# A chunked delta rule: the triangular solve folded into the tables, and four scan links a chunk in place of six

## The chip, the cores and the metric

One core of one Trainium2 chip runs the whole program. The metric is device microseconds (us) of one execution; lower is better.

## The reference, cut to what matters

The program is a block of a small network: gated experts, a delta-rule attention, gated experts, a prototype mixture, a helical attention, a prototype mixture. The change touches the delta-rule attention alone. With 2 batches of 16 heads (32 pairs), 2048 tokens and head size 16, it computes for each pair:

```python
def step(S, inp):
    qt, kt, vt, at, bt = inp
    v_hat = jnp.einsum('bij,bi->bj', S, kt)
    err = vt - v_hat
    S = at[:, None, None] * S + bt[:, None, None] * (kt[:, :, None] * err[:, None, :])
    o = jnp.einsum('bij,bi->bj', S, qt)
    return (S, o)
```

`S` is 16x16 for a pair; k and q are normalised, `at` is the decay (alpha) and `bt` the step size (beta).

## The kernel before

The tokens are cut into chunks of 8 (`CHUNK`, `C`). What depends on k, q, alpha and beta alone is computed ahead, for all chunks, in the stage `delta_chunks`; the stage `delta_recurrence` (its tiles are named `delta_scan_...`) then runs through the 256 chunks in order. Between them lies `delta_record` in DRAM, one record per chunk and pair. A record before holds five tables and a decay, 513 numbers: SOLVE (8x8, the inverse of a triangular matrix), MIX (8x8), K_IN (8x16), K_OUT (16x8), Q_IN (8x16) and the chunk's decay.

**The chunk stage.** The 128 partitions hold 2 batches x 4 parts of time x 16 heads. Each partition has 512 tokens, taken in 4 units of 128 tokens (`UNIT`); a unit has N = 16 chunks and is stored in 2 runs of 8 chunks. Per unit:

- SP loads k and q of the next unit (16 DMAs) once ACT has turned those of this one, and then stores the records, 8 DMAs a run.
- ACT turns k and q to token order (L1665), copies k to PSUM (`k_bank`, L1673), later copies SOLVE and the decay into the record.
- The scalar products of each token's k or q with the earlier k of its chunk are made by rows (w, t): w is 0 for k and 1 for q, t the token; the row has t + w products of 16 numbers for each of 16 chunks, so 256 (t + w) elements. GpSimd (POOL) multiplies 11 of the 15 rows (L1606) into three slots of `terms`; DVE sums each into `gram` (L1708), and multiplies and sums the other 4 rows itself, with k from `k_bank`.
- POOL also makes K_IN and Q_IN (L1651). DVE makes the decay products `g` (L1704, 8 small instructions), K_OUT (L1736), the triangular inverse (`invert`, L1746 to L1755) and MIX (L1760).

**The scan.** The partitions hold 2 batches x 64, four partitions of a head with 4 columns of S each (`JQ`). 32 rounds of 8 chunks; a hardware loop (`Fori`) runs over pairs of rounds. DVE runs the chain: 6 links a chunk, each in two lanes (halves of the columns) that alternate, so 12 instructions:

- links 0 and 1: product of K_IN with the state (L1949), sum with the value to `error` (L1961);
- links 2 and 3: product of SOLVE with `error`, sum to `u` (L1965);
- links 4 and 5: product of K_OUT with `u`, sum with the decayed state to the new `state` (L1969).

A link of one lane waits for the link before it of the same lane (the semaphore `chain`). Beside it ACT makes the decayed state that the last link adds (L1893), copies the state (L1896) and `u` (L1898) to SBUF for POOL, and in the sixth chunk of a round (`LOOK = 5`) copies out the outputs of the round before (L1885). POOL makes 512 products for the output from the state and Q_IN (L1931), 256 from `u` and MIX (L1935), and adds the 24 terms of an output in pairs to 12 (L1942, `o_halves`). When a round is done, PE adds those 12 with 12 matmuls against the identity (L1867; the profile records each f32 matmul as two instructions). SP loads the round after next once the round is done, and stores the outputs.

A stage ends with a barrier of all engines; the next one starts only then.

## Time and profile before

| | us |
|---|---|
| median of 3 runs | 5048.27 (5047.78 to 5050.8) |
| the profiled execution, its own time | 5050.58 |
| its span in the profile | 5048.8 |
| DVE busy over the span | 4012.5 |
| PE busy over the span | 3644.2 |
| ACT busy over the span | 3071.2 |
| POOL busy over the span | 2040.4 |
| mean granted TensorE clock, share of full | 0.86 |

The own time is what the runs are timed by; the span is what the profile's rows add up to. Shares of busy time are averages over stages that have different limits, so a change in one stage is read from the rows of that stage.

### The profile page before, as it was taken

What the parts mean: (1) busy time and instruction counts of PE and PEld (TensorE: products, weight loads), DVE (VectorE), ACT (ScalarE), POOL (GpSimd) and SP (SyncE); (2) the same over time, 40 slices, a digit from 0 to 9 for tenths busy, and PEclk for the clock granted to TensorE, in tenths of its full rate; (3) what the DMA queues carried; (4) which work ended last, traced back from release to release, by engine and by line L of the source; (5) the groups of instructions that cost most, each with busy time, mean ns of one, the idle gap of its engine ahead of it and who ended that gap; (6) DMA issues with size and microseconds to landing.
All of it is one profiled execution on the core that took longest, in us unless ns stands there. A gap on an engine that the chain in (4) does not pass through costs nothing. (4 is left out here: it accounts for less than half of the span.)

```text
span 5048.8 us, 65143 instructions
## 1 busy us (share of the span) xinstructions
PE 3644.2 (72%) x15374; PEld 1330.5 (26%) x15374; DVE 4012.5 (79%) x6760; ACT 3071.2 (61%) x4256; POOL 2040.4 (40%) x2075
## 2 busy tenths in 40 slices
PE   7985002322222589788859999999999999999568
PEld 3431001211221234234212222222222222222123
DVE  5536869999999566337879999999999999998352
ACT  5567212222222256334738999999999999999342
POOL 1000657777777211111733444444444444444112
PEclk9998556666666799899979999999999999999789
DMA  1014653433333200002450111111111111110300
GB/s 44 8 46 108 108 124 76 91 78 77 85 84 76 72 11 7 10 8 85 169 146 20 37 37 37 36 36 37 37 37 37 37 36 34 36 25 5 108 10 33
DMA packets 126522, 276.18 MB, mean 55 GB/s; under 512 B 41297, under 2 KB 70865, under 8 KB 117905
## 3 DMA queue, kind: packets, MB, share of 16 engines
q1 hardware_dynamic: 124208, 263.05, 21.8%
q10 hardware_dynamic: 1952, 9.18, 0.6%
q8 instruction: 122, 2.00, 0.2%
q14 instruction: 240, 1.96, 0.1%
HBM read 178.65 MB, written 93.36 MB: 54 GB/s over the span
## 5 line engine op out<-in xcount | busy, mean ns | idle before, releaser
L1032 POOL TENSOR_TENSOR att_heads_rest<-att_heads_probs,att_heads_high 128x352 f16<-128x352 f32 x1024 | 872.6, 852 | 1226.4 <-DVE att_heads_rest L1184 1165.9
L1164 DVE TENSOR_REDUCE att_heads_maxima<-att_heads_peek 128x1 f32<-128x1024 f32 x992 | 1210.0, 1220 | 26.4 <-PE att_heads_peek L1059 26.4
L1132 ACT ACTIVATE att_heads_probs<-att_heads_scores 128x1024 f32<-128x1024 f32 x1024 | 1057.7, 1033 | 155.1 <-PE att_heads_scores L1078 137.8
L1078 PE MATMUL att_heads_scores<-att_heads_q,att_heads_k 128*128 128x512 f16 (+1 forms) x4096 | 1072.1, 384 | 21.0 <-issue 17.5
L1134 ACT ACTIVATE att_heads_high<-att_heads_scores 128x1024 f16<-128x1024 f32 x1024 | 1056.3, 1032 | 0.0
L1184 DVE TENSOR_TENSOR att_heads_rest<-att_heads_probs,att_heads_high 128x672 f16<-128x672 f32 x1024 | 885.3, 865 | 65.7 <-POOL att_heads_rest L1032 54.5
L1867 PE MATMUL delta_scan_sums<-delta_scan_o_halves,main_identity 128*128 128x256 f32 x768 | 247.0, 496 | 952.5 <-POOL delta_scan_o_halves L1942 952.5
L1059 PE MATMUL att_heads_peek<-att_heads_k,att_heads_q 112*128 112x512 f16 x1984 | 597.8, 382 | 17.7 <-DVE att_heads_maxima L1164 14.9
L1078 PEld LDWEIGHTS att_heads_scores<-att_heads_q,att_heads_k 128*128 128x128 f16 (+1 forms) x4096 | 319.0, 98 | 691.6 <-issue 443.1
L1867 PEld LDWEIGHTS delta_scan_sums<-delta_scan_o_halves,main_identity 128*128 128x128 f32 x768 | 194.7, 259 | 1005.2 <-POOL delta_scan_o_halves L1942 965.8
L1094 PE MATMUL att_heads_out<-att_heads_high,att_heads_v_head 128*64 128x512 f16 x2048 | 418.1, 405 | 14.8 <-DVE att_heads_rest L1184 14.2
L1094 PE MATMUL att_heads_out<-att_heads_rest,att_heads_v_head 128*64 128x512 f16 x2048 | 393.6, 381 | 0.0
L259 PE MATMUL ffn_pre<-ffn_xn_parts,ffn_weights 128*128 128x512 f16 x1536 | 335.7, 382 | 11.9 <-POOL ffn_weights L298 11.9
L1931 POOL TENSOR_TENSOR delta_scan_o_terms<-delta_scan_state_copy,delta_scan_record 128x512 f32<-128x512 f32 x256 | 301.5, 1178 | 87.3 <-ACT delta_scan_state_copy L1896 87.3
L1898 ACT ACTIVATE delta_scan_u_copy<-delta_scan_banks 128x32 f32<-128x32 f32 x256 | 50.5, 197 | 436.1 <-DVE delta_scan_s_terms L1949 434.1
L341 DVE SCALAR_TENSOR_TENSOR main_x<-ffn_hidden,ffn_gate,main_x 128x512 f32<-128x512 f32 x256 | 194.9, 764 | 151.3 <-ACT ffn_hidden L284 151.3
L1893 ACT ACTIVATE delta_scan_s_terms<-delta_scan_banks,delta_scan_record 128x64 f32<-128x64 f32 x256 | 96.6, 377 | 306.0 <-DVE delta_scan_terms L1949 305.9
L1942 POOL TENSOR_TENSOR delta_scan_o_halves<-delta_scan_o_terms 128x384 f32<-128x384 f32 x256 | 256.2, 1001 | 22.7 <-POOL delta_scan_o_terms L1935 5.1
L284 ACT ACTIVATE ffn_hidden<-ffn_pre,ffn_expert 128x512 f32<-128x512 f32 x256 | 175.4, 687 | 138.7 <-PE ffn_pre L259 136.9
L1606 POOL TENSOR_TENSOR delta_chunks_terms<-delta_chunks_kq 128x256 f32<-128x256 f32 (+6 forms) x44 | 101.8, 2355 | 361.7 <-ACT delta_chunks_kq L1665 342.3
L1949 DVE TENSOR_TENSOR delta_scan_terms<-delta_scan_record,delta_scan_banks 128x256 f32<-128x256 f32 x512 | 199.6, 450 | 53.2 <-issue 39.1
L1935 POOL TENSOR_TENSOR delta_scan_o_terms<-delta_scan_u_copy,delta_scan_record 128x256 f32<-128x256 f32 x256 | 174.3, 681 | 156.0 <-ACT delta_scan_u_copy L1898 156.0
(251 smaller groups left out, 5104.3 us busy)
## 6 DMA issues: line engine op xcount, KB each, us to landing
delta_scan_record<-delta_record SPq DMA_DIRECT2D x64, 1026.0 KB, 10.7
att_heads_q<-att_hel SPq DMA_DIRECT2D x192, 128.0 KB, 3.1
att_heads_k<-att_hel SPq DMA_DIRECT2D x192, 128.0 KB, 3.2
delta_record<-delta_chunks_record SPq DMA_DIRECT2D x64, 256.5 KB, 4.7
att_hel<-att_hel_high SPq DMA_DIRECT2D x32, 512.0 KB, 4.4
att_hel<-att_hel_rest SPq DMA_DIRECT2D x32, 512.0 KB, 5.0
att_o<-att_heads_out_copy SPq DMA_DIRECT2D x256, 32.0 KB
att_out_parts<-att_o ACTq DMA_DIRECT2D x8, 1024.0 KB, 15.8
```

Of the source, the lines that this page charges most:

```text
L259: mm = nc.tensor.matmul(pre[:, k % SLOTS], weights[:, u, w_part, tile, o * P:(o + 1) * P], xn_parts[:, x_part, tile, tokens(n)], start=til ...
L1032: nc.gpsimd.tensor_tensor(rest[:, step % 4, SPLIT:], probs[:, step % 4, SPLIT:], high[:, step % 4, SPLIT:], ALU.subtract).then_inc(rest_b_ ...
L1059: mm = nc.tensor.matmul(peek[:, j], q[0:MAX_ROW, slot, 0, tile * P:(tile + 1) * P], k[0:MAX_ROW, slot, 0, tokens(part * 2 + j)], start=Tru ...
L1078: mm = nc.tensor.matmul(scores[:, step % 2, tokens(j)], k[0:rows, slot, number, tile * P:(tile + 1) * P], q[0:rows, slot, number, tokens(h ...
L1094: mm = nc.tensor.matmul(out[j * WIDE:(j + 1) * WIDE, half], v_head[:, slot, tile], part[:, step % 4, tokens(j)], start=tile == 0 and part ...
L1132: nc.scalar.activation(probs[:, step % 4], scores[:, step % 2], ACT.Exp, scale=LOGIT_SCALE).then_inc(probs_ready, 1)
L1134: nc.scalar.activation(high[:, step % 4], scores[:, step % 2], ACT.Exp, scale=LOGIT_SCALE).then_inc(high_ready, 1)
L1164: nc.vector.tensor_reduce(maxima[:, m:m + 1], peek[:].rearrange("p j n -> p (j n)"), AX.X, ALU.max).then_inc(peek_read, 1)
L1184: nc.vector.tensor_tensor(rest[:, step % 4, 0:SPLIT], probs[:, step % 4, 0:SPLIT], high[:, step % 4, 0:SPLIT], ALU.subtract).then_inc(rest ...
L1867: mm = nc.tensor.matmul(sums[:, 0:COLUMNS], c["identity"][:], o_halves[:, slot, e].rearrange("p m q -> p (m q)"), start=e == 0, stop=e == ...
L1931: nc.gpsimd.tensor_tensor(o_terms[:, m % 2, :, :, 0:HD], state_copy[:, (m - 1) % 4].unsqueeze(2).broadcast_to([P, JQ, C, HD]), table[:, Q_ ...
L1942: nc.gpsimd.tensor_tensor(o_halves[:, slot, :, m].rearrange("p e q -> p q e"), each[:, :, 0:FOLD], each[:, :, FOLD:], ALU.add).then_inc(o_ ...
```

## The change

- **Tables.** The inverse is never formed. DVE makes a table `weights` (8x8 per chunk, in PSUM): the masked and decayed products of k times beta, with minus beta on its diagonal (ACT writes the diagonal, `negated` makes the minus). K_OUT and MIX lie side by side in the record as ROWS = 16 + 8 = 24 rows of 8, and a back substitution folds the solve into both in place: for s from 7 down to 0, `fold` multiplies the columns s to 7 of all rows with `weights[s, s:]`, and `fold_sum` sums them into column s. The record has 449 numbers.
- **Who does what in the chunk stage.** POOL takes K_OUT (`k_out`) from DVE, and all 15 rows of units 1 to 3; in unit 0 DVE multiplies 3 rows (`OWN`) itself, from `kq` in SBUF. `k_bank` is gone. The row sums of unit u + 1 stand between the folds of unit u. The decays of unit u + 1 stand ahead of the folds of unit u. K_IN and Q_IN of unit u are made in the midst of the rows of unit u + 1. The last unit is folded in 2 runs, the others in one.
- **Record and queues.** `record` has two slots, each a whole unit. SP loads unit u and then stores unit u - 2.
- **Scan.** Links 2 and 3 are gone: `STEP` is 4, and K_OUT is multiplied with `error`. `error` lies in two PSUM banks. ACT copies `error` in place of `u`, once link 2 is done. POOL makes its two products straight into `o_terms[slot, 24, chunk, column, token]`, so with a stride of 256 numbers between neighbours in what it writes, and no longer adds pairs; PE adds 24 in place of 12.

The diff, cut to its core:

```diff
-SOLVE, MIX = 0, CHUNK * CHUNK
-K_IN = MIX + CHUNK * CHUNK
-K_OUT = K_IN + CHUNK * HD
-Q_IN = K_OUT + CHUNK * HD
+K_OUT = 0
+MIX = K_OUT + CHUNK * HD
+FOLDED = MIX + CHUNK * CHUNK
+K_IN = FOLDED
+Q_IN = K_IN + CHUNK * HD
...
-        record = s.sb("record", [P, RUNS, CHUNKS, RECORD])
+        fold_terms = s.sb("fold_terms", [P, N, ROWS, C])
+        record = s.sb("record", [P, 2, N, RECORD])
         gram = s.ps("gram", [P, 2, N, C, C])
-        k_bank = s.ps("k_bank", [P, UNIT, HD])
+        weights = s.ps("weights", [P, N, C, C])
...
+        OWN = ((0, C - 1), (1, C - 2), (1, C - 1))
+        def rows_of(unit):
+            if unit == 0:
+                return [(w, t) for w in range(2) for t in range(1 - w, C) if (w, t) not in OWN]
+            return [(w, t) for t in range(C) for w in range(2) if w == 1 or t >= 1]
+        def runs_of(unit):
+            return [slice(0, N)] if unit + 1 < UNITS else [slice(run * CHUNKS, (run + 1) * CHUNKS) for run in range(RUNS)]
...
                 load(0)
+                for unit in range(1, UNITS):
+                    sp.wait_ge(turned, unit * 2)
+                    load(unit)
+                    if unit >= 2:
+                        store(unit - 2)
+                for unit in range(UNITS - 2, UNITS):
+                    store(unit)
...
+                def k_out(unit):
+                    pool.wait_ge(g_step, (unit + 1) * C)
+                    record_free(pool, unit)
+                    nc.gpsimd.tensor_tensor(folded(unit, slice(0, N))[:, :, 0:HD].rearrange("p m i s -> p m s i"), by_chunk(kq[:, unit % 2, 0]),
+                                            g[:, unit % 2, :, C, 1:].unsqueeze(3).broadcast_to([P, N, C, HD]), ALU.mult).then_inc(k_out_ready, 1)
...
+                    for k, (w, t) in enumerate(rows_of(unit)):
+                        multiply_row(unit, k, w, t)
+                        if unit >= 1 and k in (4, 8):
+                            inputs(unit - 1, 0 if k == 4 else 1)
+                    k_out(unit)
...
+                def tables(unit):
...
+                    nc.vector.tensor_tensor(low, low, g[:, unit % 2, :, 1:C, 1:C], ALU.mult).then_inc(low_ready, 1)
+                    record_free(dve, unit)
+                    nc.vector.tensor_tensor(folded(unit, slice(0, N))[:, :, HD:], gram[:, 1], g[:, unit % 2, :, 1:, 1:], ALU.mult).then_inc(mix_ready, 1)
...
+                    nc.vector.tensor_tensor(weights[:, :, 0:C - 1, 1:], low.rearrange("p n t s -> p n s t"),
+                                            beta[:, :, 0:C - 1].unsqueeze(3).broadcast_to([P, N, C - 1, C - 1]), ALU.mult).then_inc(weights_ready, 1)
+                def fold(unit, run, s):
...
+                    nc.vector.tensor_tensor(out[:, :, :, s:], whole[:, :, :, s:],
+                                            weights[:, chunks, s, s:].unsqueeze(2).broadcast_to([P, count, ROWS, C - s]), ALU.mult).then_inc(fold_step, 1)
+                def fold_sum(unit, run, s):
...
+                    nc.vector.tensor_reduce(folded(unit, chunks)[:, :, :, s], fold_terms[:, chunks, :, s:], AX.X, ALU.add).then_inc(fold_step, 1)
...
                 for unit in range(UNITS):
+                    more = unit + 1 < UNITS
+                    tables(unit)
+                    if more:
                         decays(unit + 1)
+                    for run in range(len(runs_of(unit))):
+                        for s in range(C - 1, -1, -1):
+                            fold(unit, run, s)
+                            if more:
+                                row_sum(unit + 1, 2 * (C - 1 - s))
+                            if s < C - 1:
+                                fold_sum(unit, run, s)
+                            if more and s >= 1:
+                                row_sum(unit + 1, 2 * (C - 1 - s) + 1)
...
-        STEP = 6
+        STEP = 4
...
-                        for e in range(FOLD):
-                            mm = nc.tensor.matmul(sums[:, 0:COLUMNS], c["identity"][:], o_halves[:, slot, e].rearrange("p m q -> p (m q)"),
-                                                  start=e == 0, stop=e == FOLD - 1)
+                        for e in range(HD + C):
+                            mm = nc.tensor.matmul(sums[:, 0:COLUMNS], c["identity"][:], o_terms[:, slot, e].rearrange("p m j t -> p (m j t)"),
+                                                  start=e == 0, stop=e == HD + C - 1)
...
-                            wait_chains(act, number * STEP + C0 + 5)
-                            nc.scalar.activation(u_copy[:, m % 4], u[:, m % 2], ACT.Copy).then_inc(u_copied, 1)
+                            wait_chains(act, number * STEP + C0 + 3)
+                            nc.scalar.activation(error_copy[:, m % 4], error[:, m % 2], ACT.Copy).then_inc(error_copied, 1)
...
-                            ins = product(u_terms[:, m % 2, js], table[:, SOLVE:SOLVE + C * C], error[:, m % 2, js], C, C)
-                        elif at == 3:
-                            ins = nc.vector.tensor_reduce(u[:, m % 2, js], u_terms[:, m % 2, js], AX.X, ALU.add)
-                        elif at == 4:
-                            ins = product(s_terms[:, m % 2, js, :, 0:C], table[:, K_OUT:K_OUT + C * HD], u[:, m % 2, js], HD, C)
+                            ins = product(s_terms[:, m % 2, js, :, 0:C], table[:, K_OUT:K_OUT + C * HD], error[:, m % 2, js], HD, C)
```

## Rows read from the trace of the kernel before

**Rows 1.** Windows: stretch, its length, busy us of each engine (instructions), clock, DMA.
```profile
520.49:698.14 177.65, 0.00 (x0) 0.00 (x0) 165.35 (x192) 37.92 (x26) 133.11 (x60) 0.50 0.56 107
698.14:721.50 23.36, 0.00 (x0) 0.00 (x0) 0.00 (x1) 0.20 (x2) 0.00 (x0) 0.50 0.83 180
721.50:736.00 14.50, 0.00 (x0) 0.00 (x0) 0.17 (x2) 0.10 (x1) 0.00 (x0) 0.50 0.94 202
736.00:1675.60 939.60, 239.31 (x744) 188.69 (x744) 900.49 (x3072) 195.34 (x927) 720.65 (x767) 0.61 0.36 78
1675.60:1688.70 13.10, 7.69 (x24) 6.04 (x24) 0.00 (x0) 0.38 (x1) 1.34 (x2) 0.76 0.05 10
```

**Rows 2.** Timeline of DVE in the scan: start, length, and what ran.
```profile
764.17 0.79 DVE L1949 TENSOR_TENSOR delta_scan_terms<-delta_scan_record,delta_scan_banks 128x256 f32<-128x256 f32 x2
764.83 0.82 DVE L1961 TENSOR_REDUCE delta_scan_banks<-delta_scan_terms 128x16 f32<-128x272 f32 x2
765.52 0.52 DVE L1949 TENSOR_TENSOR delta_scan_u_terms<-delta_scan_record,delta_scan_banks 128x128 f32<-128x128 f32 x2
...
766.30 0.78 DVE L1949 TENSOR_TENSOR delta_scan_s_terms<-delta_scan_record,delta_scan_banks 128x256 f32<-128x256 f32 x2
766.96 0.86 DVE L1969 TENSOR_REDUCE delta_scan_banks<-delta_scan_s_terms 128x32 f32<-128x288 f32 x2
767.68 0.79 DVE L1949 TENSOR_TENSOR delta_scan_terms<-delta_scan_record,delta_scan_banks 128x256 f32<-128x256 f32 x2
...
795.18 0.75 DVE L1949 TENSOR_TENSOR delta_scan_terms<-delta_scan_record,delta_scan_banks 128x256 f32<-128x256 f32 x2 [2.79 <-issue]
```

**Rows 3.** Groups by form, the scan on POOL: busy, mean ns of one, idle before.
```profile
L1931 POOL TENSOR_TENSOR delta_scan_o_terms<-delta_scan_state_copy,delta_scan_record 128x512 f32<-128x512 f32 x256 | 301.5, 1178 | 87.3 <-ACT delta_scan_state_copy L1896 87.3
L1942 POOL TENSOR_TENSOR delta_scan_o_halves<-delta_scan_o_terms 128x384 f32<-128x384 f32 x255 | 255.2, 1001 | 22.6 <-POOL delta_scan_o_terms L1935 5.1
...
L1935 POOL TENSOR_TENSOR delta_scan_o_terms<-delta_scan_u_copy,delta_scan_record 128x256 f32<-128x256 f32 x256 | 174.3, 681 | 156.0 <-ACT delta_scan_u_copy L1898 156.0
```

**Rows 4.** Timeline of ACT and POOL in the scan.
```profile
765.05 0.38 ACT L1893 ACTIVATE delta_scan_s_terms<-delta_scan_banks,delta_scan_record 128x64 f32<-128x64 f32 x1 [1.19 <-DVE delta_scan_terms L1949]
...
767.17 0.20 ACT L1898 ACTIVATE delta_scan_u_copy<-delta_scan_banks 128x32 f32<-128x32 f32 x1 [1.70 <-DVE delta_scan_s_terms L1949]
```

**Rows 5.** Timeline of PE, and windows over one burst (instructions cut by an edge count twice).
```profile
765.80 7.65 PE L1867 MATMUL delta_scan_sums<-delta_scan_o_halves,main_identity 128*128 128x256 f32 x24 [280.56 <-POOL delta_scan_o_halves L1942]
...
771.00:773.60 2.60, 2.45 (x12) 1.81 (x10) 2.60 (x10) 0.43 (x2) 2.52 (x3) 1.00 1.08 219
```

**Rows 6.** Groups by form, the chunk stage.
```profile
L1606 POOL TENSOR_TENSOR delta_chunks_terms<-delta_chunks_kq 128x1792 f32<-128x1792 f32 x8 | 31.7, 3989 | 0.0
L1651 POOL TENSOR_TENSOR delta_chunks_record<-delta_chunks_kq,delta_chunks_g 128x1024 f32<-128x1024 f32 x16 | 31.6, 2020 | 0.0
...
L1708 DVE TENSOR_REDUCE delta_chunks_gram<-delta_chunks_own_terms 128x128 f32<-128x2048 f32 x4 | 9.1, 2285 | 0.0
...
L1752 DVE TENSOR_TENSOR delta_chunks_solve_terms<-delta_chunks_solve,delta_chunks_gram 128x784 f32<-128x784 f32 x4 | 6.2, 1554 | 0.1
...
L1708 DVE TENSOR_REDUCE delta_chunks_gram<-delta_chunks_terms 128x64 f32<-128x1024 f32 x4 | 4.9, 1223 | 0.0
```

**Rows 7.** Timeline of DVE and POOL in unit 0 of the chunk stage.
```profile
520.49 2.13 DVE L1704 TENSOR_TENSOR delta_chunks_g<-delta_chunks_g,delta_chunks_ab 128x16 f32<-128x16 f32 x8 [16.43 <-DMA delta_chunks_ab<-delta_ab]
...
551.39 2.35 DVE L1736 TENSOR_TENSOR delta_chunks_record<-delta_chunks_k_bank,delta_chunks_g 128x1024 f32<-128x1024 f32 x2
...
554.53 5.43 DVE L1747 TENSOR_SCALAR delta_chunks_solve<-delta_chunks_ab 128x128 f32<-128x128 f32 x1
...
557.20 2.62 POOL L1606 TENSOR_TENSOR delta_chunks_terms<-delta_chunks_kq 128x256 f32<-128x256 f32 x3
```

**Rows 8.** One line's instructions: count, shortest, median and longest ns, first and last start.
```profile
L1747 DVE TENSOR_SCALAR delta_chunks_solve<-delta_chunks_ab x4: 905/920/5429, 554.5 to 686.2; 128x128 f32<-128x128 f32 x4
```

**Rows 9.** Timeline of SP's queue: the stores of one unit.
```profile
570.65 19.16 SPq L1630 DMA_DIRECT2D delta_record<-delta_chunks_record  x16
```

More of the change, by code:

```diff
@@ L1568, in delta_chunks @@
     C = CHUNK
+    ROWS = HD + C
     with Scope(nc, stage) as s:
@@ L1587, in delta_chunks @@
+        decay_copied, in_ready = s.sem("decay_copied"), s.sem("in_ready")
+        stored = [s.sem(f"stored{slot}") for slot in range(2)]
         SLOTS = 3
-        rows = [(w, t) for t in range(C) for w in range(2) if w == 1 or t >= 1]
-        own_rows = [(0, 3), (1, 3), (0, 5), (1, 7)]
-        pool_rows = [row for row in rows if row not in own_rows]
-        POOLED, OWNED = len(pool_rows), len(own_rows)
         LOADS = B * PARTS * 16
-        SOLVED = 3 + 2 * (C - 1)
+        FOLDS = 2 * C - 1
@@ L1595, in places, with folded @@
+        def folded(unit, chunks):
+            return record[:, unit % 2, chunks, 0:FOLDED].rearrange("p m (r s) -> p m r s", s=C)
         def places():
@@ L1602, in by_chunk, with record_free @@
             return tile.rearrange("p (m u) i -> p m u i", u=C)
[L1604 to L1606 removed]
+        def record_free(queue, unit):
+            if unit >= 2:
+                queue.wait_ge(stored[unit % 2], unit // 2 * RUNS * LOADS)
         with nc.Block() as block:
@@ L1656, in _ @@
+                for unit in range(UNITS):
+                    for k, (w, t) in enumerate(rows_of(unit)):
[3 more added lines that the diff above has]
+                    k_out(unit)
+                for w in range(2):
+                    inputs(UNITS - 1, w)
             @block.scalar
@@ new lines, in fold @@
+                def fold(unit, run, s):
+                    chunks = runs_of(unit)[run]
+                    count = chunks.stop - chunks.start
+                    last = s == C - 1
+                    before = (unit + run) * FOLDS + 2 * (C - 1 - s) - (0 if last else 1)
+                    if last:
+                        dve.wait_ge(diagonal_ready, unit + 1)
+                        dve.wait_ge(mix_ready, unit + 1)
+                        dve.wait_ge(k_out_ready, unit + 1)
+                    if before:
+                        dve.wait_ge(fold_step, before)
+                    whole = folded(unit, chunks)
+                    out = whole if last else fold_terms[:, chunks]
+                    nc.vector.tensor_tensor(out[:, :, :, s:], whole[:, :, :, s:],
+                                            weights[:, chunks, s, s:].unsqueeze(2).broadcast_to([P, count, ROWS, C - s]), ALU.mult).then_inc(fold_step, 1)
```

235 lines of the change are left out of this document (92 added, 143 removed).

## The prediction

> **What bounds the kernel now.** I read three views. First the windows [rows 1], since the change touches two stages that stand between barriers, and what it is worth is read in them. The chunk stage runs from 520.49, when the last table has landed, to 698.14 on DVE, which is busy for 165.35 of these 177.65 us; POOL has 133.11. Then come 23.36 us in which only stores drain, 14.50 in which the scan's first loads land, 939.60 of scan with DVE busy for 900.49, and 13.10 behind DVE's last link. So both stages go by DVE, and an edit counts by what it adds to or takes from DVE's queue, unless another engine becomes later than DVE.
>
> Second, the timeline of DVE inside the scan [rows 2]. The reader is to see the pitch, not the length: two lanes overlap, so a pair of 0.79 us is followed by the next pair after 0.66. The six pairs start 0.66, 0.69, 0.78 (both SOLVE links together), 0.66 and 0.72 apart, 3.51 us a chunk, with no gap. Only at the hardware loop does DVE pause, 2.79 us with the releaser "issue"; 16 pairs of rounds have 15 of these.
>
> Third, the prices in the chunk stage [rows 6]: a DVE sum of 2048 takes 2285 ns and of 1024 takes 1223, so 1.04 ns an element and about 0.16 fixed; back to back the fixed part is 0.07 (two K_OUT products of 1024 in 2.35 us [rows 7]), and about 0.2 where an instruction waits for the one ahead. POOL pays 3989 ns for 1792, 2.2 an element, and 2020 for 1024 in K_IN and Q_IN.
>
> **The scan.** Removed: links 2 and 3 in both lanes, 765.52 to 766.30 [rows 2], 0.78 us. 256 chunks: 199.7 us. The pitch becomes 2.73. The others keep theirs if the link ahead of the same lane is still done in time: it lasts about 0.45 and the lane comes round after 0.66.
>
> What could now be late is checked against 2.73 us. ACT: the decayed state starts 0.88 us after the chunk's first link and takes 0.38 [rows 4], ready at 1.26, and the new link 3 needs it at 2.01. POOL: it loses 1.00 us of adds and keeps 1.18 + 0.68 = 1.86 [rows 3]. Its products now go out with a stride of 256 numbers. That has a near row: `o_halves` wrote with such a stride, and 384 elements took 1.00, where 256 and 512 elements give 0.93 between them. So 1.9 to 2.1 us a chunk, hidden under DVE. PE: a round's burst grows from 24 recorded instructions to 48. The first 24 took 7.65 us, and the last 11 of these 2.45 at a granted clock of 1.00 (2.4 GHz), 0.22 each [rows 5]. So 48 take 7.65 + 24 x 0.22 = 13.0. The burst begins some 0.7 us into the next round (POOL's second product ends 3.4 us after the start of the last chunk, at a pitch of 2.73) and ends at 13.7. ACT comes to the copy-out behind the sixth chunk's `error` copy, at 5 x 2.73 + 2.4 = 16.1 (link 2 ends 2.14 into a chunk, and the copy takes 0.20 [rows 4]). Hidden, with 2.4 us to spare. Loads have a round of 21.8 us and need some 14 [rows 1]. Taken: -199.7.
>
> Behind the last link nothing covers PE: 5.4 us more there, less POOL's 1.0. Taken: +4.4. The first load is 449/513 of its size: -1, out of 14.50.
>
> **The chunk stage.** DVE loses the inverse, K_OUT, and four rows a unit; it gains the folds. Fold products have 24 rows x 16 chunks = 384 times 1 to 8 elements, 13824, and the sums 384 times 2 to 8, 13440. That is 27264 x 1.04 = 28.3 us a unit, and 15 instructions at 0.1 (row sums between them hide part of the wait): 29.8. Row sums of units 1 to 3: 64 x 256 = 16384 elements, 17.0 + 15 x 0.07 = 18.1. `tables`, 784 + 1024 + 784 elements: 2.9. Decays 2.1 [rows 7]. Sum: 52.9 a unit on DVE.
>
> POOL per unit: 16384 x 2.2 = 36.0 for the rows, and three tables of 2048 at 2 x 2.02: 12.1. 48 in all, less than DVE, but with only three slots and 4 us of K_IN or Q_IN put behind rows 4 and 8, DVE comes to the row behind each too early: following both queues by these prices gives two waits of 2 us. So 57 a unit.
>
> Unit 0: DVE is free at 522.6. It sums 42 x 256 = 10752 elements of POOL's rows (12.0) and multiplies and sums 22 x 256 = 5632 of its own (11.7 + 1.2); POOL needs 2.2 an element, so DVE waits some 5 us in rows of 4 to 6 tokens. `tables(0)` begins at about 552.5; before, DVE reached this point at 551.39 [rows 7]. Three units: 723.5. The last unit has 30 half-sized fold instructions with nothing between: 28.3 + 30 x 0.2 + 2.9 + 0.4 for ACT's diagonal = 37.6. DVE ends at 761, 63 later than 698.14.
>
> The drain: 16 stores took 19.16 us [rows 9], 1.20 each, 1.05 at the new size. The first run's 8 go out under the second run's 17 us of folding, so 8.4 remain, and the 23.36 - 19.16 = 4.2 that were left behind the last issue. The stage ends at 773.7 against 721.5: +52. The earlier stores and loads have a whole unit to land in. The removed `k_bank` copies lie on ACT, which is idle for most of the stage: nothing.
>
> **Where the pages bear.** The solve product reads the inverse with a step of 8 numbers, and 784 elements took 1554 ns [rows 6], 1.8 an element against 1.04. The Trainium skill ("Advanced Engine Details and Errata", SBUF Cachelines) states that full speed needs subsequent accesses on the same 16-byte line, at least two; this row agrees. By it the folds, whose runs are contiguous but for s = 7, keep the price taken, and only about 0.6 us a unit comes on top.
>
> One short DVE instruction stood for 5.43 us, while the median of its kind is 0.92 [rows 8]; it ended at 559.96, as POOL's last queued row did, 559.82 [rows 7]. It had waited across the boundary of two POOL instructions. The Trainium skill ("SBUF — State Buffer", two separate sides) names an exclusive port pair for DVE instructions with two SBUF inputs or in a two-port mode against GpSimd. That would speak against this change: `own_row` and the decays read two SBUF tensors, the former now without `k_bank`, the latter now beside POOL's K_OUT and first rows. No row before shows two such tensor inputs held up.
>
> **Sum.** 52 - 1 - 199.7 + 4.4 = -144.3 us. The profiled execution's own time is 5050.6, so 4906.3; the median of the runs shown is 2.3 lower: 4904.
>
> **Rivals.**
> - *The folds cost what the solve product cost.* They read PSUM with the same kind of broadcast. At 1.8 in place of 1.04 on 13824 x 4 elements: +42, 4946. Against it: the scan's products broadcast PSUM vectors too, at 0.33 for 256 [rows 2].
> - *DVE is held off by POOL.* At `own_row` 1 and 2 and at three sets of decays DVE waits until POOL runs dry. After POOL's last row of a unit it has K_OUT, 4 us, and three rows, 2.7; DVE arrives after 5.1 us. So 2 us a unit, 6 if the strided K_OUT takes double, and 4 to 8 in unit 0: +10 to +25, 4922.
> - *PE becomes late.* If the clock stayed at 1.2 GHz, 13 instructions in the first 5.2 us [rows 5] give 0.40 each, 19.2 for 48; ACT is held until 19.9, and link 3 of the seventh chunk, due at 18.4, gets its term at 20.7: 2.3 x 32 = 74 us, 4978. But the clock rose within the burst.
> - *POOL takes over the scan (not faster).* Its two products set the pitch if they need more than 2.73 us; the gain is gone when they need 2.73 + 144/256 = 3.29, 1.8 times the 1.86 of today. At double price, 3.72, the scan takes 253 us more: 5157. The one strided write that the trace has costs 8%, not 80%.
> - *The chunk stage is cheaper*: no POOL waits (-12) and the folds fully back to back (-6): 4886.
>
> **How the numbers follow.** Forecast (4886 to 4916) 0.66; held off by POOL 0.13; folds at solve price 0.10; cheaper than 4886 0.05; PE late 0.03; POOL bound 0.03. The range for 8 in 10 leaves out the last two and half of the cheap case: 4880 to 4950. A measurement of this kernel tells a change of about 0.2%, 10 us, from none. All cases but the last lie far below: faster 0.96, same 0.01, slower 0.03.
>
> **What would show it.** Scan window 200 us shorter, pitch 2.73, no DVE wait for ACT or POOL; POOL's 512 product under 1.3 us; `copy_out` not waiting for PE; bursts near 13 us. Fold of 3072 elements near 3.3 us, and DVE's last sum near 761. Wrong would be: DVE groups with POOL or ACT as releaser in the scan, fold rows above 1.1 ns an element, or units longer than 60 us.

## The result, and the profile after

The kernel after takes 4886.59 us (median of 4 runs, 4884.72 to 4886.68) against 5048.02 (median of 4, 5043.45 to 5050.8) beside it: ratio 0.968, 95% interval 0.9663 to 0.9697, 161.4 us less. The forecast was 4904, with 4880 to 4950 as its range. The profiled execution's own time is 4886.68 and its span 4884.9, 163.9 below the span before.

First the windows over the same five stretches as before (columns as in [rows 1]).

```profile
520.54:763.60 243.06, 0.00 (x0) 0.00 (x0) 223.65 (x182) 27.68 (x16) 180.82 (x66) 0.50 0.44 79
763.60:776.46 12.86, 0.00 (x0) 0.00 (x0) 0.01 (x1) 0.00 (x0) 0.00 (x0) 0.50 0.73 144
776.46:789.86 13.40, 0.00 (x0) 0.00 (x0) 0.17 (x2) 0.12 (x1) 0.00 (x0) 0.50 0.94 204
789.86:1489.00 699.14, 399.97 (x1488) 330.38 (x1488) 699.06 (x2048) 195.48 (x927) 474.82 (x512) 0.76 0.43 92
1489.00:1506.16 17.16, 12.72 (x48) 10.56 (x48) 0.00 (x0) 0.39 (x2) 0.42 (x1) 0.86 0.04 8
```

The chunk stage with its drain ends at 776.46 where it ended at 721.50, so 55.0 later (forecast 52). The first load is 1.1 shorter (forecast 1), the end behind the last link 4.1 longer (forecast 4.4). The scan is 699.14 long against 939.60: 240.5 less, where the forecast had 199.7. At the barrier behind it the kernel is 1688.70 - 1506.16 = 182.5 us ahead.

The further 40 us of the scan are seen on DVE's timeline, at a place where the hardware loop closes; it answers to [rows 2].

```profile
830.17 0.81 DVE L1995 TENSOR_REDUCE delta_scan_banks<-delta_scan_s_terms 128x32 f32<-128x288 f32 x2
830.89 0.74 DVE L1979 TENSOR_TENSOR delta_scan_terms<-delta_scan_record,delta_scan_banks 128x256 f32<-128x256 f32 x2
831.55 0.78 DVE L1991 TENSOR_REDUCE delta_scan_banks<-delta_scan_terms 128x16 f32<-128x272 f32 x2
832.24 0.74 DVE L1979 TENSOR_TENSOR delta_scan_s_terms<-delta_scan_record,delta_scan_banks 128x256 f32<-128x256 f32 x2
832.90 0.81 DVE L1995 TENSOR_REDUCE delta_scan_banks<-delta_scan_s_terms 128x32 f32<-128x288 f32 x2
833.69 0.75 DVE L1979 TENSOR_TENSOR delta_scan_terms<-delta_scan_record,delta_scan_banks 128x256 f32<-128x256 f32 x2
```

Four pairs take 0.66, 0.69, 0.66 and 0.72, so 2.73 us a chunk, as forecast. The loop closes between 832.90 and 833.69, and this step is 0.79 where it is 0.72 elsewhere. Of the 2.79 us with the releaser "issue" (time in which the engine waited for nothing that the profile shows) that stood there before, nothing is left. The 15 pauses before were 2.49 to 2.81 us long, 39.1 in all, as the group of that line in the trace before has it:

```profile
L1949 DVE TENSOR_TENSOR delta_scan_terms<-delta_scan_record,delta_scan_banks 128x256 f32<-128x256 f32 x512 | 199.6, 450 | 53.2 <-issue 39.1 <-DMA delta_scan_vt<-delta_v 14.1
```

The groups by form of the scan show whether another engine came near DVE (against [rows 3]); the second half of a row is idle time before it.

```profile
L1967 POOL TENSOR_TENSOR delta_scan_o_terms<-delta_scan_state_copy,delta_scan_record 128x512 f32<-128x512 f32 x256 | 304.6, 1190 | 284.1 <-ACT delta_scan_state_copy L1932 284.1
L1979 DVE TENSOR_TENSOR delta_scan_terms<-delta_scan_record,delta_scan_banks 128x256 f32<-128x256 f32 x512 | 189.0, 409 | 13.0 <-DMA delta_scan_vt<-delta_v 13.0
L1971 POOL TENSOR_TENSOR delta_scan_o_terms<-delta_scan_error_copy,delta_scan_record 128x256 f32<-128x256 f32 x256 | 177.0, 691 | 1.9
...
L1921 ACT ACTIVATE delta_scan_o_out<-delta_scan_sums 128x256 f32<-128x256 f32 x32 | 12.3, 384 | 13.7 <-PE delta_scan_sums L1903 13.7
```

DVE waits for nothing but the first load. POOL writes with the stride of 256 at 1190 and 691 ns, where the dense writes took 1178 and 681: 1 to 1.5% more. ACT waits for PE once, 13.7 us, behind the last round. PE's bursts in its timeline, against [rows 5]:

```profile
812.42 13.32 PE L1903 MATMUL delta_scan_sums<-delta_scan_o_terms,main_identity 128*128 128x256 f32 x48 [327.27 <-POOL delta_scan_o_terms L1971]
834.26 12.65 PE L1903 MATMUL delta_scan_sums<-delta_scan_o_terms,main_identity 128*128 128x256 f32 x48 [8.52 <-POOL delta_scan_o_terms L1971]
```

In ACT's timeline the copy-out of this round begins at 827.71, 2 us behind 812.42 + 13.32 = 825.74.

The chunk stage on DVE's timeline, against [rows 7] and [rows 8]:

```profile
522.59 2.02 DVE L1749 TENSOR_TENSOR delta_chunks_fold_terms<-delta_chunks_kq 128x1792 f32<-128x1792 f32 x1
...
538.27 2.94 DVE L1749 TENSOR_TENSOR delta_chunks_fold_terms<-delta_chunks_kq 128x1792 f32<-128x1792 f32 x1
...
553.88 0.98 DVE L1762 TENSOR_TENSOR delta_chunks_gram<-delta_chunks_gram,delta_chunks_g 128x784 f32<-128x784 f32 x1
...
556.79 3.06 DVE L1733 TENSOR_TENSOR delta_chunks_g<-delta_chunks_g,delta_chunks_ab 128x16 f32<-128x16 f32 x8
...
569.71 0.96 DVE L1740 TENSOR_REDUCE delta_chunks_gram<-delta_chunks_terms 128x48 f32<-128x768 f32 x1 [2.04 <-POOL delta_chunks_terms L1666]
...
611.80 0.97 DVE L1762 TENSOR_TENSOR delta_chunks_gram<-delta_chunks_gram,delta_chunks_g 128x784 f32<-128x784 f32 x1
...
614.69 2.12 DVE L1733 TENSOR_TENSOR delta_chunks_g<-delta_chunks_g,delta_chunks_ab 128x16 f32<-128x16 f32 x8
...
761.85 1.75 DVE L1791 TENSOR_REDUCE delta_chunks_record<-delta_chunks_fold_terms 128x192 f32<-128x1536 f32 x1
```

`tables(0)` begins at 553.88 (forecast 552.5), `tables(1)` 57.9 later (forecast 57), the last sum ends at 763.60 (forecast 761). Its prices by form, against [rows 6]:

```profile
L1666 POOL TENSOR_TENSOR delta_chunks_terms<-delta_chunks_kq 128x1792 f32<-128x1792 f32 x6 | 23.8, 4009 | 0.0
L1672 POOL TENSOR_TENSOR delta_chunks_record<-delta_chunks_kq,delta_chunks_g 128x2048 f32<-128x2048 f32 x4 | 15.7, 3936 | 0.0
...
L1784 DVE TENSOR_TENSOR delta_chunks_fold_terms<-delta_chunks_record,delta_chunks_weights 128x3072 f32<-128x3072 f32 x3 | 10.0, 3343 | 0.0
```

And the waits of DVE for POOL's rows in this stage (total, times, longest). Two of about 2 us stand in each of the units 1 to 3, 12.4 us in all, and the other three, 4.5 us, in unit 0:

```profile
DVE delta_chunks_gram L1740 <- POOL delta_chunks_terms L1666: 16.9, 9, 2.1
```

SP's queue, against [rows 9], has the last 48 stores in one piece, whose end is the end of the stage:

```profile
668.94 102.79 SPq L1642 DMA_DIRECT2D delta_record<-delta_chunks_record  x48
```

**What was lost again.** 182.5 us ahead at the barrier and 163.9 at the end: 18.6 us went in stages that the change doesn't touch. One tile that is made 32 times, from the head attention's start to near its end (the view of one tile: shortest, median, longest ns, first and last start), bounds the place. Before:

```profile
L1169 DVE TENSOR_REDUCE att_heads_tile_max<-att_heads_maxima x32: 186/186/188, 2634.7 to 4638.9; 128x16 f32<-128x32 f32 x32
```

After:

```profile
L1169 DVE TENSOR_REDUCE att_heads_tile_max<-att_heads_maxima x32: 185/186/188, 2455.7 to 4477.8; 128x16 f32<-128x32 f32 x32
```

That is 2004.2 and 2022.1, 17.9 us more (the stretch between the scan and this one is 3.5 longer, the end 2.8 shorter). The groups of PE say what ended its idle time. Before:

```profile
L1078 PE MATMUL att_heads_scores<-att_heads_q,att_heads_k 128*128 128x512 f16 (+1 forms) x4096 | 1072.1, 384 | 21.0 <-issue 17.5 <-DMA att_heads_q<-att_heads_shift_row 2.2 <-ACT att_heads_high L1134 1.3
```

After:

```profile
L1078 PE MATMUL att_heads_scores<-att_heads_q,att_heads_k 128*128 128x512 f16 (+1 forms) x4096 | 1075.2, 385 | 32.1 <-issue 28.8 <-DMA att_heads_q<-att_heads_shift_row 2.2 <-ACT att_heads_high L1134 1.1
```

The time with the releaser "issue" grew by 11.3 us: before it stands in six places, one at each close of the attention's loop (2.63 to 3.22 us), and after in twelve, two at each close (2.79 to 3.31, then 1.34 to 2.25). One of the closes in PE's timeline after:

```profile
2738.14 0.38 PE L1094 MATMUL att_heads_out<-att_heads_rest,att_heads_v_head 128*64 128x512 f16 x2
2741.84 0.82 PE L1078 MATMUL att_heads_scores<-att_heads_q,att_heads_k 128*128 128x512 f16 x3 [3.31 <-issue]
2744.87 0.61 PE L1078 MATMUL att_heads_scores<-att_heads_q,att_heads_k 113*128 113x512 f16 x1 [2.21 <-issue]
...
2747.26 1.89 PE L1078 MATMUL att_heads_scores<-att_heads_q,att_heads_k 128*128 128x512 f16 x4
...
2750.47 1.04 PE L1078 MATMUL att_heads_scores<-att_heads_q,att_heads_k 128*128 128x512 f16 x4
```

The same place before:

```profile
2916.29 0.38 PE L1094 MATMUL att_heads_out<-att_heads_rest,att_heads_v_head 128*64 128x512 f16 x2
2919.55 1.04 PE L1078 MATMUL att_heads_scores<-att_heads_q,att_heads_k 128*128 128x512 f16 x4 [2.88 <-issue]
...
2922.15 1.89 PE L1078 MATMUL att_heads_scores<-att_heads_q,att_heads_k 128*128 128x512 f16 x4
...
2925.05 1.04 PE L1078 MATMUL att_heads_scores<-att_heads_q,att_heads_k 128*128 128x512 f16 x4
```

Before, one stop of 2.88; after, the first matmuls of the pass are cut by a second stop of 2.21. From the last matmul ahead of the stop to the third group of scores it was 8.76 us and is 12.33: 3.57 more, of which 2.64 are stops. Over six closes the 17.9 us are 3.0 each. The rest is the clock: behind the stops the granted clock is at 1.2 GHz (0.52 of full from 2746 to 2750), and four matmuls take 1.89 in place of 1.04. The longer break keeps PE at that level for more of its matmuls than before: `att_heads_peek` (L1059) behind these four still takes 1.05 us after, and 0.74 before.

### The profile page after: what moved, and what is told of

The parts are those of the page before. It is cut to its first block and busy times, and to the rows that moved or that the text cites. A ratio compares the mean times of both kernels' runs of the same rounds, so it can differ in the third digit from the quotient of the medians.

```text
span 4884.9 us, 64394 instructions
## 1 busy us (share of the span) xinstructions
PE 3811.3 (78%) x16142; PEld 1479.4 (30%) x16142; DVE 3865.6 (79%) x5725; ACT 3062.1 (63%) x4245; POOL 1846.0 (38%) x1828
## 5 line engine op out<-in xcount | busy, mean ns | idle before, releaser
L1903 PE MATMUL delta_scan_sums<-delta_scan_o_terms,main_identity 128*128 128x256 f32 x1536 | 412.7, 437 | 604.4 <-POOL delta_scan_o_terms L1971 604.4
L1059 PE MATMUL att_heads_peek<-att_heads_k,att_heads_q 112*128 112x512 f16 x1984 | 599.9, 383 | 18.2 <-DVE att_heads_maxima L1164 17.1
L1903 PEld LDWEIGHTS delta_scan_sums<-delta_scan_o_terms,main_identity 128*128 128x128 f32 x1536 | 340.9, 224 | 676.5 <-POOL delta_scan_o_terms L1971 617.6
L1967 POOL TENSOR_TENSOR delta_scan_o_terms<-delta_scan_state_copy,delta_scan_record 128x512 f32<-128x512 f32 x256 | 304.6, 1190 | 284.1 <-ACT delta_scan_state_copy L1932 284.1
L1666 POOL TENSOR_TENSOR delta_chunks_terms<-delta_chunks_kq 128x256 f32<-128x256 f32 (+7 forms) x57 | 139.6, 2489 | 349.8 <-ACT delta_chunks_kq L1702 319.2
L1094 PEld LDWEIGHTS att_heads_out<-att_heads_high,att_heads_v_head 128*64 128x64 f16 x2048 | 112.2, 106 | 456.5 <-issue 422.0
L1059 PEld LDWEIGHTS att_heads_peek<-att_heads_k,att_heads_q 112*128 112x128 f16 x1984 | 130.7, 97 | 334.0 <-DVE att_heads_maxima L1164 328.6
L259 PEld LDWEIGHTS ffn_pre<-ffn_xn_parts,ffn_weights 128*128 128x128 f16 x1536 | 151.1, 98 | 195.5 <-issue 17.1
L1995 DVE TENSOR_REDUCE delta_scan_banks<-delta_scan_s_terms 128x32 f32<-128x288 f32 x512 | 207.3, 449 | 0.0
```

The source lines that it names most:

```text
L259: mm = nc.tensor.matmul(pre[:, k % SLOTS], weights[:, u, w_part, tile, o * P:(o + 1) * P], xn_parts[:, x_part, tile, tokens(n)], start=til ...
L1059: mm = nc.tensor.matmul(peek[:, j], q[0:MAX_ROW, slot, 0, tile * P:(tile + 1) * P], k[0:MAX_ROW, slot, 0, tokens(part * 2 + j)], start=Tru ...
L1094: mm = nc.tensor.matmul(out[j * WIDE:(j + 1) * WIDE, half], v_head[:, slot, tile], part[:, step % 4, tokens(j)], start=tile == 0 and part ...
L1903: mm = nc.tensor.matmul(sums[:, 0:COLUMNS], c["identity"][:], o_terms[:, slot, e].rearrange("p m j t -> p (m j t)"), start=e == 0, stop=e ...
L1967: nc.gpsimd.tensor_tensor(o_terms[:, slot, 0:HD, m].rearrange("p e j t -> p j t e"), state_copy[:, (m - 1) % 4].unsqueeze(2).broadcast_to( ...
L1995: ins = nc.vector.tensor_reduce(state[:, m % 4, js], s_terms[:, m % 2, js], AX.X, ALU.add)
```

## The experiments

Two things were to be explained that the prediction had taken as fixed: DVE's pause at the loop, gone (39 us), and PE's new stops (18 us). Then the terms that it had sized: the o-terms without halving, the queue order, the two runs. Each kernel ran beside the kernel before on its chip; that one took 5057.31 us beside scan_only, the two with pad128 and halves_kept, 5066.46 beside the two loop_plus, before_pe_pad96 and after_pool_pad25, and 5045.3 beside after_pe_pad160, inputs_later and one_run. The stretches between these stages, which no edit touches, differ by up to 10 us between these traces (from the last `att_heads_tile_max` to the end of the span it is 406.2 to 416.2), so what is compared are the windows: chunk stage, scan, and first to last `att_heads_tile_max`. A single time is quoted for orientation.

**scan_only: the new scan on the chunk stage of before.** `delta_recurrence` is that of the kernel after; the record keeps its old layout and the chunk stage its work.

```diff
-                nc.vector.memset(g[:], 1.0).then_inc(zeroed, 1)
+                nc.vector.memset(g[:], 0.0).then_inc(zeroed, 1)
...
-        STEP = 6
+        STEP = 4
```

> The kernel before with the scan of the changed kernel alone (four links, PE adding 24 terms); the chunk stage and the record of 513 numbers stay as before. The solve is left out of the recurrence and the decay products are zeroed, so the output is not the reference's; the instructions and their shapes are. Theory A, the pause of 2.8 us at DVE's hardware loop is independent of the links: pitch 2.73, scan 200 us shorter, 4 us more behind it, about 4853 us in all. Theory B, the pause goes with the shorter loop body (214 instructions in place of 310): 240 us shorter, about 4813 us. By either the chunk stage ends at 698.

Measured: 4835.59 us. The chunk stage ends as before (the scan's load starts at 720.4), the scan takes 699.1 us, and the group of its first product has no "issue":

```profile
L1939 DVE TENSOR_TENSOR delta_scan_terms<-delta_scan_record,delta_scan_banks 128x256 f32<-128x256 f32 x512 | 188.9, 408 | 13.0 <-DMA delta_scan_vt<-delta_v 13.0
```

The attention takes 2021.1. So both surprises come with the scan's change alone, and the chunk stage has no part in either. The total lies 23 us above theory B's 4813, which had no term for the longer attention.

**before_pad128 and after_pad128: DVE's code moved by 128 instructions.** Small memsets in the chunk stage, ahead of the scan.

```diff
+        pad = s.sb("pad", [P, 128])
...
+                for i in range(128):
+                    nc.vector.memset(pad[:, i:i + 1], 0.0)
```

> The kernel before with 128 one-column memsets on DVE ahead of the chunk stage's own memsets, where DVE then waits for DMA for 16 us. They move DVE's later instructions by half of 256. Theory B, only the length of the loop body counts: the 15 pauses of 2.8 us in the scan stay, the scan takes 940 us, and the total is 5048 within 10. Theory C, what counts is where the body of the loop lies in the instruction stream: the pauses change or vanish (up to 42 us less), and the pauses in the head attention move too, by up to 20 us either way.

> The changed kernel with the same 128 memsets on DVE ahead of the chunk stage. Theory B: no pause in the scan, 699 us for it, total 4887 within 8. Theory C: the pauses of the scan come back, 15 of 2 to 3 us, scan near 740 us, and the head attention may change by up to 20 us either way.

Measured: 5051.96 and 4892.58 us. The scan's first product, before with the memsets:

```profile
L1952 DVE TENSOR_TENSOR delta_scan_terms<-delta_scan_record,delta_scan_banks 128x256 f32<-128x256 f32 x512 | 189.1, 409 | 52.7 <-issue 39.3 <-DMA delta_scan_vt<-delta_v 13.4
```

The pauses stay, 39.3 us, and after has none still (scan 939.8 and 699.4). The attention keeps its 1999.2 and 2021.2. Where DVE's code lies, by half of 256, decides neither.

**loop_plus32 and loop_plus96: the body of DVE's loop made longer again.** Semaphore increments that nobody waits for, 2 or 6 in each of the 16 chunks of a pass.

```diff
+                            for _ in range(2):      # 6 in loop_plus96
+                                dve.sem_inc(pad, 1)
```

> The changed kernel with 32 more DVE instructions in the loop body of the scan (2 semaphore increments a chunk, nothing waits for them). Theory B, the pause comes with a loop body beyond some length between 214 and 310 listed instructions: either no pause (then the bound is above 246) or 15 pauses of 2.8 us, 40 us in the scan. If the increments cost DVE time, the pitch of 2.73 us grows by some 0.1.

> The changed kernel with 96 more DVE instructions in the loop body of the scan (6 semaphore increments a chunk), so as many as the kernel before had there. Theory B: 15 pauses of 2.8 us are back with the releaser issue, scan 40 us longer than 699, and pitch 2.73 if the increments are hidden. Rival D, the pause belongs to the SOLVE links or to PE and POOL beside them and not to the body's length: no pause, scan 699.

Measured: 4893.59 and 4985.41 us; scans of 701.8 and 790.1. The group with 32 more:

```profile
L1980 DVE TENSOR_TENSOR delta_scan_terms<-delta_scan_record,delta_scan_banks 128x256 f32<-128x256 f32 x512 | 188.0, 405 | 14.9 <-DMA delta_scan_vt<-delta_v 13.4 <-issue 0.2
```

With 96 more, the group and one pause in the timeline:

```profile
L1980 DVE TENSOR_TENSOR delta_scan_terms<-delta_scan_record,delta_scan_banks 128x256 f32<-128x256 f32 x512 | 192.4, 417 | 71.9 <-issue 59.7 <-DMA delta_scan_vt<-delta_v 12.0
...
836.18 0.75 DVE L1980 TENSOR_TENSOR delta_scan_terms<-delta_scan_record,delta_scan_banks 128x256 f32<-128x256 f32 x2 [3.99 <-issue]
```

The pause is back, 3.80 to 4.18 us in 15 places. A pass of DVE's loop has 310 instructions in the listing of the program before and 214 after, waits counted (the traces record only the working ones, 3072 / 16 = 192 and 2048 / 16 = 128): the pause is there at 310 (before) and at 214 + 96, and not at 214 or 246. So a longer body brings the pause, and Rival D, which tied it to the SOLVE links, is out. The scan is 91 us longer in place of the expected 40. The pauses are 59.7 of these, and the pitch within a round, 2.81, is 20. The last 11.1 are a second stop of 0.79 to 1.04 us, again with the releaser "issue", in the fourth chunk of 12 of the 16 passes. The kernel before has no such second stop, and its pauses are a third shorter at the same count of instructions. So the count alone doesn't set how long DVE stops; what else does isn't shown.

**before_pe_pad96, after_pool_pad25, after_pe_pad160: PE's or POOL's code moved.** With the change a round has 24 recorded matmuls and 24 weight loads more on PE, 96 instructions for the two rounds in the loop's body, and POOL's code is shorter. These insert increments ahead of the scan's loop, on one engine.

```diff
+                for _ in range(96):      # in before: on pe
+                    pe.sem_inc(pad, 1)
...
+                for _ in range(25):      # in after: on pool
+                    pool.sem_inc(pad, 1)
...
+                for _ in range(160):     # in after: on pe
+                    pe.sem_inc(pad, 1)
```

> The kernel before with 96 instructions (semaphore increments) on PE ahead of the scan's loop: they move PE's later code as the 24 added f32 matmuls (four recorded instructions each) of the change do. Theory P, the head attention's 18 to 20 us come from where PE's loop lies: heads window 2021 us in place of 2004. Theory Q, they come from POOL's code, which the change moved by 25 listed instructions, or from something else: 2000 to 2004.

> The changed kernel with 25 semaphore increments on POOL ahead of the scan's loop, which put POOL's later code back to where it was before the change. Theory Q: heads window back to 2000 to 2004 us from 2022, total about 4866. Theory P: 2022, total 4885 to 4893.

> The changed kernel with 160 semaphore increments on PE ahead of the scan's loop. With the 96 instructions that the change added they move PE's later code by 256 from where it lay before. Theory P with a period of 256 instructions: heads window back from 2022 to 2000 to 2004 us, total about 4866. Rival, the place matters but not with that period: the window stays at 2022, or goes elsewhere.

Measured: 5066.53, 4882.48 and 4874.68 us. The last is 9 us above the expected 4866, which lies in the stretches that nobody edited (the one behind the attention is 6.4 us longer than in the kernel after). The attention takes 2021.4 us in before with PE's code moved by 96 (2637.0 to 4658.4), 2022.1 in after with POOL's moved (2452.3 to 4474.4), and 2004.9 in after with PE's moved by 160 (2454.5 to 4459.4). PE's groups agree. Before, moved by 96:

```profile
L1078 PE MATMUL att_heads_scores<-att_heads_q,att_heads_k 128*128 128x512 f16 (+1 forms) x4096 | 1075.7, 385 | 31.3 <-issue 27.9 <-DMA att_heads_q<-att_heads_shift_row 2.2 <-ACT att_heads_high L1134 1.2
```

After, moved by 160:

```profile
L1078 PE MATMUL att_heads_scores<-att_heads_q,att_heads_k 128*128 128x512 f16 (+1 forms) x4096 | 1072.7, 384 | 20.7 <-issue 17.3 <-DMA att_heads_q<-att_heads_shift_row 2.2 <-ACT att_heads_high L1134 1.1
```

The stops can be given to the kernel before and taken from the one after by instructions that do nothing in the attention. The cause is the place of PE's code, and with 160 more ahead of it the kernel after has the attention of before. All fourteen traces of this case fall in line: where PE's code lies as before, or 256 instructions on, the attention takes 1997.7 to 2004.9 us (five kernels), and where it lies 96 on, 2019.5 to 2022.8 (nine). The Trainium skill ("Runtime: NRT & Kernel Launch", Instruction fetch mechanics) says that instructions are fetched in blocks of 256 and that a taken branch to a target outside the two blocks at hand stalls. PE's response to its place and the return with 96 + 160 = 256 agree with blocks of 256, though no other shift was tried, and a pause that comes with a longer body agrees with the rule on branches. That DVE's pause didn't answer to a shift of 128 isn't explained by it, and no run here looks at a fetch itself: as the reason for either stop it is argued and not shown.

**halves_kept: POOL adds the halves again.** The third POOL instruction of before is put back, PE adds 12.

```diff
-                        for e in range(HD + C):
+                        for e in range(FOLD):
...
+                            pool.wait_ge(o_terms_ready, number * 2 + 2 + TERMS_CREDIT)
+                            nc.gpsimd.tensor_tensor(o_halves[:, slot, :, m].rearrange("p e q -> p q e"), each[:, :, 0:FOLD], each[:, :, FOLD:],
+                                                    ALU.add).then_inc(o_halves_ready, 1)
```

> The changed kernel with POOL's third instruction per chunk put back: it adds the 24 terms in pairs, and PE adds 12. If POOL's queue would bound a four-link scan, POOL needs 1.18 + 0.68 + 1.00 us and the waits between, so the pitch is 2.9 to 3.1 us in place of 2.73 and the scan 40 to 100 us longer, 4930 to 4985 us in all; DVE's rows show waits whose releaser is ACT or POOL. Rival, POOL's queue has slack: pitch 2.73, total 4885, and 5 us less behind the last link as PE's burst is half as long.

Measured: 4894.46 us. Scan 722.7, 22.6 behind its last link, attention 2001.1. POOL's three products need 1178 + 1002 + 682 ns = 2.86 us a chunk, more than 2.73, and the engine is busy through:

```profile
L1969 POOL TENSOR_TENSOR delta_scan_o_terms<-delta_scan_state_copy,delta_scan_record 128x512 f32<-128x512 f32 x256 | 301.6, 1178 | 61.7 <-ACT delta_scan_state_copy L1934 61.7
L1980 POOL TENSOR_TENSOR delta_scan_o_halves<-delta_scan_o_terms 128x384 f32<-128x384 f32 x256 | 256.4, 1002 | 22.7 <-POOL delta_scan_o_terms L1973 5.1
```

Without the second half of the change POOL would be the bound, as expected, but the scan is only 23.6 us longer and not 40 to 100. POOL's lag reaches DVE in the copy-out: ACT waits there for PE, 39.0 us in 24 rounds and 19.0 behind the last link, and makes the decayed state late, for which DVE waits 33 times:

```profile
DVE delta_scan_banks L2003 <- ACT delta_scan_s_terms L1931: 20.5, 33, 1.6
```

By these prices POOL needs 256 x (2.86 - 2.73) = 33 us more than DVE. The scan has 23.6 of them, and the end behind its last link, 22.6 against the 13.1 that a burst of 24 took before, has the other 9.5. In the own time the loss is only some 8 us, since this kernel leaves PE's code as it was and so keeps the short attention. That bears the place of PE's code out once more.

**inputs_later: K_IN and Q_IN behind POOL's rows 9 and 13.**

```diff
-                        if unit >= 1 and k in (4, 8):
-                            inputs(unit - 1, 0 if k == 4 else 1)
+                        if unit >= 1 and k in (9, 13):
+                            inputs(unit - 1, 0 if k == 9 else 1)
```

> The changed kernel with K_IN and Q_IN made behind rows 9 and 13 in place of 4 and 8. If DVE's waits in rows 5 and 9 are there because 4 us of POOL's work stand ahead of these rows while the rows are short, both waits go, one shorter wait may come behind row 13: units of 53 to 54 us in place of 57.0, DVE's end of the stage 8 to 11 us earlier, near 753. Rival, the later turn of k and q by ACT, which waits for these tables, holds up POOL's next rows: no gain or a loss of a few us.

Measured: 4871.54 us. The stage ends at 765.4 in place of 776.5, 1.1 of this because the tables landed at 519.4. DVE's last sum ends at 752.5, as expected. The waits:

```profile
DVE delta_chunks_gram L1740 <- POOL delta_chunks_terms L1666: 7.0, 6, 1.9
```

16.9 became 7.0. The two waits a unit of the prediction are there, and they come from the place of those 4 us in POOL's queue, since moving them alone takes them away. Of the 7.0, 4.5 are those of unit 0, which the edit leaves as they were.

**one_run: the last unit folded in one run.**

```diff
-            return [slice(0, N)] if unit + 1 < UNITS else [slice(run * CHUNKS, (run + 1) * CHUNKS) for run in range(RUNS)]
+            return [slice(0, N)]
```

> The changed kernel with the last unit folded in one run, not two. DVE has 15 instructions less at 0.2 us, so it ends 3 us earlier, near 760.5; but all 16 stores then go out behind it, 8 more at 1.05 us: the stage's end, 776.5 now, comes 5 us later. Rival, the stores drain in parallel with one another and the end stays.

Measured: 4901.2 us. DVE ends at 760.5, 3 us sooner, but all 16 stores stand behind it, and the scan's load starts at 782.1 in place of 776.5: +5.7. (The other 9 us of the total lie in the stretches between the stages.) Hence the half of the stores that goes out under the second run is worth what the prediction gave it.

**best: inputs_later and PE's code moved by 160, together.**

> The changed kernel with both: K_IN and Q_IN behind rows 9 and 13, and 160 semaphore increments on PE ahead of the scan's loop. If the two gains are independent: the chunk stage 10 us shorter (DVE's end near 753), heads window 2004 us, so 27 to 28 us less than the changed kernel, 4857 to 4862 us, ratio to the kernel before 0.962 to 0.964. Rival, one of the two was chance between executions: 4870 to 4877.

Measured, over 5 runs: 4855.74 us (4851.91 to 4861.31) against 5055.06 (9 runs, 5043.8 to 5063.8): ratio 0.9605, 95% interval 0.9588 to 0.9622. The chunk stage ends at 767.4, the scan takes 699.2, the attention 1997.7:

```profile
L1169 DVE TENSOR_REDUCE att_heads_tile_max<-att_heads_maxima x32: 185/186/188, 2451.0 to 4448.7; 128x16 f32<-128x32 f32 x32
```

That is 30.9 us less than the kernel after, where 27 to 28 were expected, and just below the expected range of 4857 to 4862. The kernel after did not run beside it, but its ratio to the kernel before, 0.968 (0.9663 to 0.9697), lies wholly above this one, so this kernel beats both.

## Why the prediction was right, and where it was wrong

**Direction, mechanism and range: right.** The sum was -144.3 and the spans differ by -163.9. By stages: +52 was +55.0, -1 was -1.1, -199.7 was -240.5, +4.4 was +4.1, and 0 elsewhere was +18.6.

**Step that failed first: "Only at the hardware loop does DVE pause, 2.79 us".** The prediction read the pause, counted 15, and left it in the scan's new length. The shorter loop body took all 39.1 us away. With them taken off, the scan would have been forecast at 939.6 - 199.7 - 39.1 = 700.8; it took 699.1. None of the rivals covered it. loop_plus96 brought the pause back at a body of the old length.

**Step that failed second: what lies outside the two stages keeps its time.** PE's longer code in the scan moved all PE code behind it, and the attention's loop took 17.9 more. This had no term and no rival. The two errors of opposite sign, -39 and +18.6, leave the 20 us by which the sum was off. The first alone would have put the total 39 us from the forecast, so that the second halved it is luck, and by itself the agreement of the total would have said little.

**The links: right.** Pitch 2.73. 256 chunks without the link's 0.78 are the 199.7. POOL has 1.88 us of products a chunk (forecast 1.9 to 2.1), its 512 product takes 1.19 (forecast under 1.3), DVE waits for neither POOL nor ACT, PE's bursts are 12.65 and 13.32 (forecast 13.0) and end 2 us ahead of the copy-out (forecast 2.4). The rivals "PE becomes late" and "POOL takes over" didn't happen; halves_kept shows how near the second was, with 2.86 against 2.73 if the adds had stayed.

**The chunk stage: right, each term a little low.** Unit 0 +1.4, three units 171.8 for 171, the last unit 37.9 for 37.6, the drain 12.9 for 12.6: 2.8 in all. The fold of 3072 took 3.34 (forecast near 3.3), 1.09 ns an element with its fixed part. So the folds don't cost what the solve product cost, and that rival is out. The one with s = 7, which reads and writes with a step of 8 numbers, does:

```profile
L1784 DVE TENSOR_TENSOR delta_chunks_record<-delta_chunks_record,delta_chunks_weights 128x384 f32<-128x384 f32 x3 | 2.5, 834 | 0.0
```

At 1.04 an element and 0.16 fixed, 384 would take 560: the step costs 0.27 us a unit. The Trainium skill's rule ("Advanced Engine Details and Errata", SBUF Cachelines), cited in the prediction, agrees in direction. The prediction's "about 0.6 us a unit" doesn't follow from its own prices: 384 x (1.8 - 1.04) is 0.29, and that is what the trace has.

**The rival "held off by POOL": there, but small.** `own_row` of 1792 took 2.02 us at 522.59, with POOL not yet begun, and 2.94 at 538.27 beside it; the one of 2048 took 3.30 at 545.17, some 1.0 more than [rows 6] have for a sum of 2048. The 8 decays took 3.06 at 556.79 against 2.12 at 614.69. Together 2.9 us, and not 10 to 25. What happened is seen when POOL's own instructions are set beside them:

```profile
537.54 1.80 POOL L1666 TENSOR_TENSOR delta_chunks_terms<-delta_chunks_kq 128x768 f32<-128x768 f32 x1
539.30 4.13 POOL L1666 TENSOR_TENSOR delta_chunks_terms<-delta_chunks_kq 128x1024 f32<-128x1024 f32 x1
```

POOL's spans are rough, but these fit to about 0.1 us. DVE's product of 538.27 came while POOL's row of 768 ran, which ended at 539.34. Counted from there, 2.0 us more lead to the product's end at 541.21: it stood for about 1 us and then ran at its usual length. POOL's next row took 4.13 us where the same size takes 2.36 in a later unit, and 2.36 counted back from its end, 543.43, is 541.07: it stood until DVE's product was done. The product of 545.17 shows the same, with a row of 1536 at 5.47 in place of 3.49. So the two engines took turns, each held until the other's instruction ended. That it is a shared port of the memory which they pass on is argued; the rows show the turns. The 5.43 of [rows 8] was another thing: that instruction, with one tensor input, stood from 554.53 through the ends of POOL instructions at 555.30, 557.26, 557.94 and 558.61, not one boundary as the prediction has it, and POOL's had their usual lengths. That it let four turns go by, and the two-input products none, is what made the rival's price of 10 to 25 us too high; why isn't shown.

**Left open.** Where between 246 and 310 instructions the bound on the body lies and what sets it, why the pause is 2.6 us in one body of 310 and 4.0 in another, why it doesn't answer to a shift of 128, and which places of PE's code are good ones, beyond the two that were tried.

## What to carry to other kernels

When an edit shortens or lengthens a loop's body, "issue" time at the loop's end isn't a constant of the kernel: count the body's instructions and give the pause a term of its own. Before two kernels are compared, look at one stage that neither touches; if it moved, suspect the place of the code, and a few idle instructions ahead of it show in one run whether it is the cause. When a term is saved on the bounding engine, work out the sum of each other engine per chunk as well: here POOL's 2.86 against DVE's 2.73 would have cost 33 us without the second half of the change. And the order within a queue counts: moving 4 us of POOL's work was worth another 10.

## What the runs showed of the hardware

- DVE stopped 2.49 to 2.81 us at each close of a loop of 310 listed instructions, and 3.80 to 4.18 with 214 and 96 increments; at 214 and 246 it didn't stop. 128 instructions ahead of it changed nothing (39.3 us of stops against 39.1).
- In a loop that had not been edited PE got a second stop, of 1.34 to 2.25 us, behind the first when its code lay 96 instructions further on, and lost it with 160 more: 2022.1, 2021.4 against 2004.2, 2004.9 us for the stage. Behind the stop it ran at the 1.2 GHz level: four matmuls of 512 columns in 1.89 us, then 1.04.
- GpSimd wrote f32 with a stride of 256 numbers at 1190 ns for 512 elements, dense at 1178.
- A DVE product of two operands in SBUF, 1792 elements, took 2.02 us alone and 2.94 when it came while a GpSimd product ran; GpSimd's next product, of 1024, took 4.13 in place of 2.36. Each stood until the other's was done. A DVE instruction with one tensor input stood for 5.43 us, through four ends of GpSimd instructions.
